# The skip term of a state-space scan: from VectorE operations to TensorE matmuls with diagonal matrices

## What is computed

```
xz = x @ in_proj_w + in_proj_b
xc, z = split(xz);  xc = silu(causal_conv4(xc))
delta_s, B, u = split(xc @ x_proj_w + x_proj_b)
delta = softplus(delta_s @ dt_proj_w + dt_proj_b)
h[t, d, n] = exp(-(n + 1) * delta[t, d]) * h[t-1, d, n] + delta[t, d] * B[t, n] * u[t, d]
y = sum over n of h
y = y + u * D
y = y * silu(z)
x = x + y @ out_proj_w + out_proj_b
```

## Time and profile before

| | us |
|---|---|
| device time, median of 3 runs | 1258.98 |
| lowest and highest | 1255.26 to 1262.06 |
| device time of the profiled execution | 1254.54 |
| its span | 1252.5 |
| busy: PE, PEld | 1112.3, 592.8 |
| busy: DVE, ACT, POOL | 934.7, 783.2, 327.7 |

### The profile page before, as it was taken

How to read it: one execution, slowest core, us unless ns; L and a number is a source line. 1 busy time by engine, 2 the same in 40 slices (tenths; PEclk the granted TensorE clock), 3 DMA queues, 4 the chain that set the end, 5 groups by cost and what they waited for, 6 DMA issues and landing times.

```text
span 1252.5 us, 15950 instructions
## 1 busy us (share of the span) xinstructions
PE 1112.3 (89%) x5645; PEld 592.8 (47%) x5704; DVE 934.7 (75%) x1739; ACT 783.2 (63%) x1156; POOL 327.7 (26%) x271
## 2 busy tenths in 40 slices
PE   5889876888998999989999899999979789799998
PEld 2455453343333333333332288887633334357776
DVE  4788766967888888888863178887789999984442
ACT  4777631455665656656678898667758677455554
POOL 4233431111100000000011221211169788840000
PEclk9789988999999999999999999999989999899999
DMA  5211563346000000000000131211223222200000
GB/s 150 78 43 69 129 150 77 81 103 139 2 2 1 2 1 2 1 1 1 2 19 10 32 119 60 85 49 36 86 81 113 85 110 92 102 1 3 6 9 18
DMA packets 30623, 67.29 MB, mean 54 GB/s; under 512 B 3952, under 2 KB 16240, under 8 KB 28496
## 3 DMA queue, kind: packets, MB, share of 16 engines
q1 hardware_dynamic: 30544, 66.27, 18.5%
HBM read 57.47 MB, written 8.78 MB: 53 GB/s over the span
## 4 chain that ended last, share of the span: by engine, by line
PE 54%; DVE 15%; POOL 9%; issue 9%; ACT 7%; DMA 1%; SPq 0%; DVEq 0%; POOLq 0%; ACTq 0%
PE psum L1347 8%; PE psum L405 7%; PE psum L407 7%; PE psum L406 7%; DVE mx L1244 7%; PE psum L1232 7%; PE psum L1301 6%; POOL drive L2136 6%; DVE hst L2158 2%; ACT probs L1315 2%; PE psum L473 1%; PE psum L539 1%; PE psum L547 1%; ACT edec L634 1%; ACT psum L2090 1%
## 5 line engine op out<-in xcount | busy, mean ns | idle before, releaser
L1244 DVE TENSOR_REDUCE mx<-psum 128x1 f32<-128x512 f32 (+3 forms) x640 | 349.2, 604 | 63.0 <-PE psum L1232 30.4
L1315 ACT ACTIVATE probs<-psum 128x1024 f32<-128x1024 f32 (+1 forms) x320 | 283.4, 936 | 169.2 <-PE psum L1301 140.0
L1232 PE MATMUL psum<-kz,qa 128*128 128x512 bf16 (+3 forms) x605 | 189.9, 352 | 24.7 <-DVE mx L1244 17.3
L1301 PE MATMUL psum<-qa,kz 128*128 128x512 bf16 (+1 forms) x616 | 169.0, 359 | 9.7 <-DMA qa<-m_rows 4.3
L1347 PE MATMUL psum<-probs,v 128*32 128x512 f32 (+3 forms) x1280 | 150.5, 541 | 2.1 <-POOL probs L1326 1.4
L2136 POOL TENSOR_TENSOR drive<-du,b_bc 128x1024 f32<-128x1024 f32 x64 | 149.6, 2370 | 10.6 <-DVE hx_lo L671 9.1
L1232 PEld LDWEIGHTS psum<-kz,qa 128*128 128x128 bf16 x640 | 56.9, 97 | 185.4 <-DVE mx L1244 137.4
L2077 PE MATMUL psum<-hst,ident 128*128 128x512 f32 x256 | 123.0, 626 | 20.6 <-DVE u L2176 14.1
L1326 POOL TENSOR_SCALAR_AFFINE_SELECT probs<-probs 128x512 f32<-128x512 f32 x48 | 29.3, 634 | 357.1 <-ACT probs L1315 357.1
L2158 DVE TENSOR_TENSOR_SCAN hst<-psum,hlast,drive 128x512 f32<-128x512 f32 x96 | 115.3, 1263 | 8.9 <-ACT psum L2090 5.0
L671 DVE TENSOR_TENSOR hx_lo<-hid,hx_hi 128x1024 fp32r<-128x1024 f32 x64 | 81.4, 1276 | 33.8 <-ACT hx_hi L1673 29.7
(11 more groups left out here) (294 smaller groups left out, 1944.3 us busy)
## 6 DMA issues: line engine op xcount, KB each, us to landing
b_bc<-b_rows SPq DMA_DIRECT2D x16, 1024.0 KB, 4.7
cs_bc<-cs_rows SPq DMA_DIRECT2D x16, 512.0 KB, 4.8
gate_bc<-gate_rows SPq DMA_DIRECT2D x32, 256.0 KB, 3.2
qk_part_rows<-qk_parts SPq DMA_DIRECT2D x48, 128.0 KB, 2.3
ew_raw<-experts_dram SPq DMA_DIRECT2D x8, 512.0 KB, 3.6
qa<-qk_part_rows SPq DMA_DIRECT2D x16, 192.0 KB, 5.5
kz<-qk_part_rows SPq DMA_DIRECT2D x16, 192.0 KB, 6.1
fw_raw<-net_dram SPq DMA_DIRECT2D x11, 256.0 KB, 2.7
```

The costliest lines, as they stand in the source:

```text
L1232: ins = pe.matmul(out[:, 0:w], qa[:, b, h // 2, i * P:(i + 1) * P], key_rows(h, c)[:, 0:w], start=True, stop=not last, skip_group_check=True)
L1244: dve.tensor_reduce(mx[:, 4 * i + h % 4, c:c + 1], fill_bank("mx", k, n)[:, 0:w], AX.X, ALU.max).then_inc(S["mx_read"], 1)
L1301: ins = pe.matmul(out[:, lo:], key_rows(h, kt // TPB)[:, kt % TPB * P:(kt % TPB + 1) * P], qa[:, b, h // 2, lo:], start=True, stop=not dia ...
L1315: act.activation(probs[:, st % 2, hh, :, lo:], s_pair[n % 2][:, :, lo:], ACT.Exp, scale=SCALE).then_inc(S["p_done"], 1)
```

## The change

Three edits. ACT builds two diagonal matrices of D once, within the experts, from the identity and the column of D. PE multiplies u with them into banks 0 and 1, within the block's own group of sums, behind the sum of the third state. `scan_y_dve` loses its two skip operations, and the waits for them.

```
         fo = sb("fo", [P, 2, BLK], F32)
         assert free[0] <= W_END, (free[0], W_END)
+        d_diag = sb("d_diag", [P, 2, P], F32)
...
                 for part in MF_ACT.get(k, ()):
                     scan_front_act(o, act, 0, part)
+                if k == Y_MOVE:
+                    for j in range(2):
+                        act.activation(d_diag[:, j, :], ident[:, :], ACT.Identity, scale=C("d1", j))
...
         SUM_AFTER = 3
+        SKIP_AFTER = 2
...
                 ins = pe.matmul(bank[j][:, :], ident[:, :], hst[:, (NS1 * b + n) % HBUF, j, :], start=(n == 0), stop=(n == NS1 - 1))
             ins.then_inc(S["summed"], 1)
+            if n == SKIP_AFTER:
+
+                pe.wait_ge(S["c_u_read"], 2 * b + 2)
+                for j in range(2):
+                    pe.matmul(bank[j][:, :], d_diag[:, j, :], u1[:, b % 2, j, :], start=False, stop=False)
...
             dve.wait_ge(S["summed"], NS1 * (b + 1))
             u = u1[:, b % 2, :, :]
-            for j in range(2):
-                n = o.did(dve.scalar_tensor_tensor(bank[j][:, :], u[:, j, :], C("d1", j), bank[j][:, :], ALU.mult, ALU.add))
             dve.wait_ge(S["sz_ready"], b + 1)
             for j in range(2):
-                o.wait(n - 1 + j)
                 ins = dve.tensor_tensor(u[:, j, :], bank[j][:, :], sz1[b % 2][:, j, :], ALU.mult)
```

More of the change, by code:

```diff
@@ L331, in build @@
         assert free[0] <= W_END, (free[0], W_END)
+        d_diag = sb("d_diag", [P, 2, P], F32)
+        assert t_end["ew_hi3"] <= t_end["fo"] <= t_end["d_diag"] - 1024 and t_end["d_diag"] <= A_END
         free[0] = t_end["sz1_even"]
```

## The result

| | before | changed |
|---|---|---|
| device time, median of 18 runs each, us | 1258.47 | 1253.05 |
| lowest and highest | 1255.26 to 1262.12 | 1250.04 to 1257.65 |
| ratio, 95% interval | | 0.996, 0.9948 to 0.9973 |
| span of the profiled execution | 1252.5 | 1255.3 |

The change takes about 5.0 us off (0.4%, interval 3.4 to 6.5 us). That is less than the 0.5% (6.3 us) that the prediction took as what one measurement can tell, but the interval leaves out zero. The spans look the other way round, and this is the first thing to learn here: the second scan began at 918.67 us in the profiled execution of before and at 924.65 in that of the changed kernel, 6 us later, after work in which the change adds only the two short activations for the diagonals (priced in the last experiment).

A forecast was written before the change was run, and what follows sets the result against it. The prediction took VectorE to set the scan's pace, with TensorE bounding the network behind it. Its terms: −3.87 − 0.38 − 0.29 + 0.99 = −3.55 us, so 1258.98 − 3.55 = 1255.4 us, range 1250.0 to 1261.5.

The forecast's parts named there:

- VectorE's pair, −3.87: Scan blocks 0 to 2: dropping VectorE's two skip operations gains 1.29 us a block, 3.87 us in all.
- The clock behind y, −0.29: Blocks 1 and 2: TensorE idles only 1.9 us, its clock stays up; 0.29 us gained in block 1, nothing in block 2.
- The products in blocks 0 to 2, 0: TensorE's added diagonal products, 1.72 us a block, are hidden by slack (1.89 us in block 1); price 0.
- The products in the last block, +0.99: TensorE's queue has no gap there, so the added 1.72 us pair delays VectorE; 0.99 us lost.
- The wait at the network's third output, −0.38: Behind block 3, y comes 1.29 us earlier, so TensorE's 0.38 us wait there goes and nothing more.
- ScalarE, 0: Two activations building the diagonals, 0.86 us, fit in a 1.21 us wait of a weight split; cost nothing.
- GpSimd is the bound: Rival, scan: VectorE's gain only turns into waits for drives; loss of 0.3 us, 1259.3 us; chance 0.14.
- TensorE the bound in every block: Rival, sums behind the added pair: it costs time four times; 2.6 us slower, 9.5 at low clock; chance 0.08.
- The clock up in the last block too: Rival, last block: TensorE's clock stays up or returns at once; 6.6 us gained, 1252.4 us; chance 0.10.

The follow-up runs named there:

- the last experiment, twelfth: Kernel before plus only the two ScalarE activations that build the diagonals, used by nothing; 1258.37 us, ratio 1.0002.
- sixth: Changed kernel with six useless matmuls ahead of the last block's first sum, four before the scan, and last-block added products behind the tenth sum; 1250.87 us, ratio 0.9944.
- tenth kernel: Repeat, without further edit, of the changed kernel with both stretches of useless matmuls and late last-block products; 1249.98 us, ratio 0.9945.
- fourth: Changed kernel with the last block's added products moved behind the tenth sum, in place of the third; 1253.83 us, ratio 0.9965.
- third kernel: Changed kernel with VectorE's two skip operations put back beside the added products, so the skip term counts twice; 1258.32 us, ratio 1.0011.
- fifth: Changed kernel with six useless matmuls on TensorE ahead of the last block's first sum; 1251.24 us, ratio 0.9953.
- eleventh: Changed kernel with six useless matmuls in the last block and its added products behind the tenth sum, none before the scan; 1252.06 us, ratio 0.9953.
- seventh kernel: Changed kernel with the added pair of products issued twice in blocks 0 to 2, last block unedited; 1253.11 us, ratio 0.9967.

## Why the prediction was right

Three traces of the scan as it was (before, its second trace, the diagonals alone) and three of the changed kernel give the sum by terms. Means:

| | first state to y 0 | y 0 to 1 | y 1 to 2 | to y 3 | y 3 to end | sum |
|---|---|---|---|---|---|---|
| as before | 57.64 | 50.35 | 50.39 | 39.39 | 136.64 | 334.41 |
| changed | 56.64 | 48.72 | 48.72 | 38.93 | 137.74 | 330.75 |
| gain | 1.00 | 1.63 | 1.67 | 0.46 | −1.10 | 3.66 |

The traces give 3.66 us where the forecast had 3.55; the times give 5.0, 2.8 and 4.4, and their intervals hold it all three times. The predicted 1255.4 stands 2.35 us above the measured median: 0.5 because the kernel before had 1258.47 in the longer series and not 1258.98, the other 1.8 lie within the interval. The sum came out closer than its terms: against the forecast block 0 gave 0.29 us less and the third output 0.19 less, the clock behind y 0.43 more and the last block 0.16 more. That these nearly cancel is luck, and so is part of the 3.66 itself: the three sums of before run from 333.8 to 335.1.

- **VectorE's pair, −3.87.** Right. With the clock up in both, block 1 is 50.03 or 50.04 us with the pair and 48.72 without: 1.3 us. In block 0 the two traces of before with a low clock as long as the changed kernel's have 57.92 on the mean, 1.28 more than 56.64; the first trace, with the shorter low clock, has only 0.48 more. All 14 traces agree with this reading. Without the skip pair, block 0 took 55.5 us where the low clock ended 7.6 us behind the first state (sixth and tenth kernel), 56.4 at 9.8 us (fourth) and 56.6 to 56.8 at 10.2 to 10.6; with the pair and 1.29 us taken off, 55.8 at 7.7, and 56.5 to 56.7 at 10.1 to 10.4. Only the four matmuls at the start moved that end by an edit.
- **The clock behind y, −0.29.** The direction was right and the term too small, since it was read from one execution. What is left of blocks 1 and 2 beside 1.29 is 0.34 + 0.38 = 0.72 us. I priced block 2 at nothing, because ScalarE's decay came last there in the one trace of before that I had the earlier trace rows. In it the clock fell 1.2 us after the first sum had begun; in the other two it fell 0.7 and 0.2 us ahead of it, and then the sum comes last (50.68, 50.47). The statement that the clock stays up was right for the three traces of the changed kernel, but not in general, see below.
- **The products in blocks 0 to 2, 0.** Right: leaving them out changes nothing there, and a second pair is hidden too in blocks 0 and 2. The limit was wrong: the cover was said to end at 1.89 us, and 3.4 us stayed hidden.
- **The products in the last block, +0.99.** Right in mechanism; the size was met under the low clock of the changed kernel alone. The waits were forecast as 0.4 and 0.9 us and are 0.34 and 0.79. Leaving the products out or moving them gives 0.9 to 1.0 back, where the low clock ends 4.7 to 5.1 us behind the first sum. Where it ended at 4.0 the pair cost 0.4 (third kernel against the twelfth), and with the clock up 0.3 (fifth against the eleventh). Against the means of before the last block without its skip pair is 0.83 longer (1.29 − 0.46). The first trace of before alone would have given only 0.44, because its low clock lasted 5.6 us or a little more from the first sum on the earlier trace rows; in the other two it lasted 3.3 and 4.0, and their last block is 39.11 and 39.31. The 0.34 us at 1100.64, which the prediction calls a wait for a drive, stands in the profile without a releaser; that it is one is inferred from GpSimd's drive that began at 1098.19 and took 2.36 us. One reading of the prediction can be tested by this: the Trainium skill (Perfetto Trace Analysis, Identifying the Most-Contended Engine) judges TensorE's headroom by the share of weight loads, beside that of the peak arithmetic, and by the share of loads the pair would have been free in the last block. The measured 0.9 us speaks against taking that share as room in a queue without a gap; the same pair 14 us further back in it was free.
- **The wait at the network's third output, −0.38.** Half right: 0.19 us (1.29 − 1.10). The wait is gone, but I had priced it by the row of a weight load. Timeline of TensorE's products around it, kernel before:

```profile
1116.89 0.39 PE L407 MATMUL psum<-xT_hi,fw_hi 128*128 128x512 f32 x1
1117.24 0.50 PE L405 MATMUL psum<-xT_hi,fw_lo 128*128 128x512 f32 x1
1117.58 0.40 PE L406 MATMUL psum<-xT_lo,fw_hi 128*128 128x512 f32 x1
1117.81 0.39 PE L407 MATMUL psum<-xT_hi,fw_hi 128*128 128x512 f32 x1
```

Products start 0.23 us apart, and here twice 0.35 and 0.34: the delay is 0.23 us and not 0.38: part of the load's wait does not show in the starts of the products. An engine's wait is priced by the starts of the work behind it.
- **ScalarE, 0.** Right, by the run with the diagonals alone and by its row.

The rivals. *GpSimd is the bound:* refuted. VectorE's 1.3 us came out of each block and went back in with the two operations (third kernel), and drives are none of its waits in the changed kernel. View of VectorE's waits over the scan of the changed kernel (answers to the earlier trace rows):

```profile
DVE hst L2169 <- ACT psum L2101: 12.1, 8, 2.8
DVE hst L2169 <- PE psum L2083: 2.1, 2, 1.7
...
DVE x_tok L2200 <- PE psum L2193: 0.8, 1, 0.8
```

And yet the chain of waits over the last part of the program gives the drive more than before (20.0% in the earlier trace rows):

```profile
by line: POOL drive L2147 21.2%; PE psum L407 12.2%; PE psum L409 11.6%; PE psum L408 11.5%; issue 9.3%; DVE hst L2169 4.7%; PE psum L2083 3.1%; ACT psum L2101 2.0%; POOL fw_lo L673 2.0%; PE psum L1961 1.9%; PE psum L1956 1.7%; DVE hx_lo L6
```

Two engines that run nearly level and hand buffers to each other can both stand in such a chain. What tells them apart is who waits for whom. *TensorE the bound in every block:* refuted by the doubled products where the clock is up; where it fell, the second pair cost 0.5 us more (block 1 of the seventh kernel). *The clock up in the last block too:* it did not come by itself (the low clock lasts 4.9 us behind an idle of 6.34, and 4.1 to 5.1 in all six traces with this idle), which agrees with the low chance. Brought about by the six matmuls it is worth nearly what the rival said: 6.6 us forecast for it, 334.41 − 327.89 = 6.5 measured with them and the late place, 6.2 less what the late place gives.

## What to carry to other kernels

An operation of the engine that sets the pace is worth moving to one that is busier over the whole program, if it lands there ahead of a point with slack; the same pair cost 0 us in three blocks and 0.9 us in the fourth, where a place 14 us later in the queue made it free again. Before a stretch in which TensorE's first results are waited for, try to fill its idle time with useless matmuls on data at hand: ten of them gained 3.7 us here in the traces (326.78 against 330.75, less 0.3 for the late place), as much as the whole change. Part of it, 0.6 us, is that the added pair costs 0.3 and not 0.9 once the clock is up. And read gains of a few us from stages that start at a common event, in more than one trace of each kernel.

## What was not expected of the hardware

**The clock behind an idle of 1.9 us.** The prediction took from one place that it stays up. Over the ten traces of kernels with this idle there are 20 such places, in blocks 1 and 2, and it fell in 4 (once each in the fifth, sixth, seventh and tenth kernel). Behind an idle of 3.2 us it fell in 6 of 8, each time for 3.4 or 6.8 us. So a shorter idle makes the fall rarer and does not exclude it. The advice of the Trainium skill (TensorE: Matmul & The Clock Gate, Why this matters for your kernels) to keep the gaps between bursts of matmuls short agrees with this as a tendency. With one pair or none, the fall costs between 0 (sixth kernel, 1 us behind the first sum's start in block 2) and 0.65 us (50.68 against 50.03), by its moment.

**The stretch ahead of the scan.** The first state began between 918.67 and 924.65 us in 14 traces, though nearly all kernels are the same up to there. This is more than the change is worth. It goes with the time for which TensorE's clock was low ahead of the scan: the three traces with the least of it (47.8 us) began at 918.67 to 919.32, four with 51 to 55 us at 918.85 to 921.95, and seven with 58 us at 921.71 to 924.65. Two stretches of TensorE, from the attention and from the experts, the kernel before first and then the changed one (columns as in the earlier trace rows), show where the clock differed:

```profile
553.00:568.00 15.00, 12.84 (x80) 1.00 0.01 2
720.00:730.00 10.00, 10.00 (x53) 1.00 0.34 95
```

```profile
553.00:568.00 15.00, 12.23 (x60) 0.77 0.00 1
720.00:730.00 10.00, 8.15 (x42) 0.83 0.34 105
```

No edit changed this clock, and the traces with 58 us still differ by 2.9 us, so the cause is in part open.
